# Four of nine depthwise taps moved from VectorE to TensorE, with the batch-norm columns on GpSimd and an early exponential, in a one-core metaformer kernel

## The reference, cut to what matters

```python
x1 = jnp.transpose(x, (0, 3, 1, 2))
x1 = lax.conv_general_dilated(x1, dw_k, (1, 1), [(PAD, PAD), (PAD, PAD)], feature_group_count=C)
x1 = bn_g[:, None, None] * (x1 - bn_m[:, None, None]) * lax.rsqrt(bn_v + 1e-05)[:, None, None] + bn_b[:, None, None]
x1 = jax.nn.silu(x1)
x1 = jnp.transpose(x1, (0, 2, 3, 1))
offset = x1 @ off_w + off_b
mask = jax.nn.softmax((x1 @ mask_w + mask_b).reshape(N, H, W, G, P), -1)
...
samples = _bilinear_sample(img, sg)
m = mask.reshape(N, H * W, G, P).transpose(0, 2, 1, 3).reshape(N * G, 1, H * W, P)
out = (samples * m).sum(-1)
```

## Time and profile before

| quantity | value |
|---|---|
| median of 3 runs | 272.5 us (272.42 to 273.59) |
| the profiled execution, its own time | 271.01 us |
| its span, first to last instruction | 268.9 us |
| mean granted TensorE clock | 0.924 of full speed |

### The profile page before, as it was taken

The page is one execution under the profiler, slowest core; times in us unless marked ns, Lnnn a source line. Parts: engine busy times, 40 slices in busy tenths (PEclk is TensorE's granted clock), DMA queues, the critical chain, the costliest instruction groups (busy, mean ns, idle before and its releaser), DMA issues.

```text
span 268.9 us, 3312 instructions
## 1 busy us (share of the span) xinstructions
PE 221.1 (82%) x1200; PEld 151.8 (56%) x1200; DVE 166.4 (62%) x412; ACT 55.9 (21%) x93; POOL 113.2 (42%) x150
## 2 busy tenths in 40 slices
PE   0968469898995889979794599999999869999980
PEld 0726167778993733224432289999999444334430
DVE  6796878996758286565414999966200354325496
ACT  1221944231000165424011101010102110211000
POOL 5600007999913309710800399997300020000760
PEclk9999959999999559999998589999999995999997
DMA  3547990000000000000029200000000000000000
GB/s 92 177 115 162 204 253 24 0 0 4 1 4 0 0 1 0 0 4 0 0 73 211 49 2 0 2 0 2 0 2 0 0 1 2 0 0 0 0 20 20
DMA packets 5825, 9.58 MB, mean 36 GB/s; under 512 B 2328, under 2 KB 2992, under 8 KB 5808
## 3 DMA queue, kind: packets, MB, share of 16 engines
q1 hardware_dynamic: 5808, 9.37, 14.8%
HBM read 7.67 MB, written 1.69 MB: 35 GB/s over the span
## 4 chain that ended last, share of the span: by engine, by line
PE 58%; DVE 24%; ACT 6%; issue 5%; POOL 4%; DMA 1%; DVEq 0%; POOLq 0%; ACTq 0%
PE ps L774 19%; PE ps L963 6%; PE ps L1031 6%; PE ps L757 4%; PE ps L702 3%; PE ps L917 3%; PE ps L832 3%; DVE cm L1143 2%; DVE xn L1099 2%; PE ps L854 2%; DVE ring L301 2%; POOL big L564 2%; PE ps L710 2%; DVE stats L1088 2%; DVE ps L1196 2%
## 5 line engine op out<-in xcount | busy, mean ns | idle before, releaser
L270 POOL TENSOR_TENSOR big<-big 128x576 f32<-128x576 f32 x32 | 36.3, 1176 | 21.5 <-DVE big L293 17.9
L757 PE MATMUL ps<-ring,ident 128*128 128x192 f32 x126 | 26.0, 357 | 8.6 <-DVE ring L301 8.4
L774 PE MATMUL ps<-ident,ring 128*128 128x128 f32 x256 | 32.7, 273 | 0.0
L270 DVE TENSOR_TENSOR ring<-big,ps 128x576 f32<-128x576 f32 x40 | 27.2, 749 | 5.5 <-PE ps L774 5.3
L311 POOL TENSOR_TENSOR big<-big 128x512 f32<-128x512 f32 x27 | 29.0, 1113 | 2.5 <-ACT big L631 2.4
L757 PEld LDWEIGHTS ps<-ring,ident 128*128 128x128 f32 x126 | 22.2, 205 | 12.8 <-DVE ring L301 12.8
L447 POOL TENSOR_TENSOR rstd<-veps,mhalf 128x4 f32<-128x4 f32 x8 | 8.2, 1028 | 49.6 <-DVE veps L1095 49.5
L774 PEld LDWEIGHTS ps<-ident,ring 128*128 128x128 f32 x256 | 28.9, 141 | 0.3 <-DVE ring L311 0.2
L774 PE MATMUL ps<-ident,big 128*128 128x128 f32 x212 | 27.7, 273 | 0.1
L774 PEld LDWEIGHTS ps<-ident,big 128*128 128x128 f32 x212 | 24.2, 141 | 1.3 <-POOL big L270 0.5
L702 PE MATMUL ps<-zero,ident 128*128 128x512 f32 x34 | 21.9, 793 | 2.8 <-DVE big L1436 2.8
(11 more groups left out here) (266 smaller groups left out, 334.8 us busy)
## 6 DMA issues: line engine op xcount, KB each, us to landing
big<-pad SPq DMA_DIRECT2D x8, 392.0 KB, 9.8
big<-pad SPq DMA_DIRECT2D x8, 240.0 KB, 5.4
w<-in_w_dram SPq DMA_DIRECT2D x2, 512.0 KB
w<-in_w_dram SPq DMA_DIRECT2D x2, 256.0 KB
pad<-img SPq DMA_DIRECT2D x8, 64.0 KB, 2.1
pad<-zero SPq DMA_DIRECT2D x1, 484.0 KB, 3.7
pad<-zero SPq DMA_DIRECT2D x1, 400.0 KB, 4.5
x<-in_x_dram SPq DMA_DIRECT2D x1, 256.0 KB, 2.8
```

Of the source, the lines that this page charges most:

```text
L270: return eng.tensor_tensor(term_slot(who, k, n * K * C, [3 * C1, 3], [C1, 3], [K * C1, G1], [1, C1]), bigv(dy * SLAB1 + (dx + j) * C, [SLA ...
L757: return mm(bank(px + dx, 0, P, [1, 3 * J * G0], off=dy * J * G0), ident[:, :], ring[:, slot + 3 * px * J * G0:slot + 3 * (px + 1) * J * G ...
L774: return mm(dst, columns, ident[:, :], is_transpose=True, start=first, stop=last, skip_group_check=True)
```

## The change

Taps 5 to 8 go to TensorE, taps 0 to 4 stay on VectorE. GpSimd builds four diagonal 128x128 weights in `w_shift`, a buffer that is used only much later. TensorE accumulates four multiplications in PSUM bank 4 on shifted views of `cpad`, and VectorE adds the bank to its own sum. `keep_clock` shrinks from four to one. The three batch-norm column instructions move from VectorE to GpSimd, ahead of the four memsets. ScalarE takes a one-column exponential right behind the SiLU.

```diff
-        warm = sb("warm", P, 1)
+        warm = sb("warm", P, 2)
...
+        dw_diag = w_shift
...
             pool.wait_ge(sem("bnv"), 1)
-            gp.tensor_tensor(bn[:, 1:2], bn[:, 0:1], mhalf[:, 0:1], ALU.pow).then_inc(sem("bnr"), 1)
+            step(gp.tensor_tensor(bn[:, 1:2], bn[:, 0:1], mhalf[:, 0:1], ALU.pow))
+            pool.wait_ge(sem("ident"), 1)
+            for q, tap in enumerate(PE_TAPS):
+                gp.tensor_scalar(dw_diag[:, q, :], ident[:, :], w_dc[:, tap:tap + 1], None, ALU.mult
+                                 ).then_inc(sem("dw_diag"), 1)
+            step(gp.tensor_tensor(bn[:, 2:3], w_dc[:, K:K + 1], bn[:, 1:2], ALU.mult))
+            step(gp.tensor_tensor(bn[:, 4:5], w_dc[:, K + 2:K + 3], bn[:, 2:3], ALU.mult))
+            gp.tensor_tensor(bn[:, 3:4], w_dc[:, K + 1:K + 2], bn[:, 4:5], ALU.subtract).then_inc(sem("bn"), 1)
             for weights in (w_i1[:, :, :], cw_parts[:, :, :], oh_parts[:, :, :], b1_parts[:, :]):
                 last = gp.memset(weights, 0.0)
...
                           bias=bn[:, 3:4], scale=bn[:, 2:3]).then_inc(sem("x1T"), 1)
+            sc.activation(warm[:, 1:2], mhalf[:, 0:1], ACT.Exp).then_inc(sem("exp_table"), 1)
...
             project(w_in[:, :], 2, C, "img0_ps", 1)
+            pe.wait_ge(sem("dw_diag"), len(PE_TAPS))
+            pe.wait_ge(sem("cpad0"), 1)
+            for n, tap in enumerate(PE_TAPS):
+                ky, kx = divmod(tap, 3)
+                last = mm(bank(4, 0, P, [1, 512]), dw_diag[:, n, :],
+                          V(cpad, 0, ky * (W + 2) + kx, [[1, P], [NP0, 2], [W + 2, H], [1, W]]),
+                          start=(n == 0), stop=(n == len(PE_TAPS) - 1))
+            last.then_inc(sem("dw_ps"), 1)
             pe.wait_ge(sem("zero_set"), 1)
-            keep_clock(4, 4)
+            keep_clock(1, 5)
...
-            step(last)
+            last.then_inc(sem("cpad0"), 1)
+            dve.wait_ge(sem("cpad0"), 1)
             n_dw = 15 * (W + 2) + W
-            for tap in range(K):
+            for q, tap in enumerate(DVE_TAPS):
                 ky, kx = divmod(tap, 3)
...
-                if tap == 0:
-                    step(v.tensor_scalar(dst, src, w_dc[:, 0:1], None, ALU.mult))
-                elif tap < K - 1:
+                if q == 0:
+                    step(v.tensor_scalar(dst, src, w_dc[:, tap:tap + 1], None, ALU.mult))
+                else:
                     step(v.scalar_tensor_tensor(dst, src, w_dc[:, tap:tap + 1], dst, ALU.mult, ALU.add))
-                else:
-                    v.scalar_tensor_tensor(dst, src, w_dc[:, tap:tap + 1], dst, ALU.mult, ALU.add).then_inc(sem("dwc"), 1)
-
-            dve.wait_ge(sem("bnr"), 1)
-            step(v.tensor_tensor(bn[:, 2:3], w_dc[:, K:K + 1], bn[:, 1:2], ALU.mult))
-            step(v.tensor_tensor(bn[:, 4:5], w_dc[:, K + 2:K + 3], bn[:, 2:3], ALU.mult))
-            v.tensor_tensor(bn[:, 3:4], w_dc[:, K + 1:K + 2], bn[:, 4:5], ALU.subtract).then_inc(sem("bn"), 1)
+            dve.wait_ge(sem("dw_ps"), 1)
+            rows = V(dwc, 0, 0, [[1, P], [H * (W + 2), 2], [W + 2, H], [1, W]])
+            v.tensor_tensor(rows, rows, bank(4, 0, P, [256, 2], [W, H], [1, W]), ALU.add).then_inc(sem("dwc"), 1)
...
+PE_TAPS = (5, 6, 7, 8)
+DVE_TAPS = (0, 1, 2, 3, 4)
```

## The result

The changed kernel takes 269.32 us (median of 4, 268.3 to 269.69) against 272.46 (median of 4): ratio 0.9876, interval 0.9844 to 0.9907. That is 3.1 us by the medians, where 2.7 and 269.8 us were forecast. Between the two profiled executions only 2.0 us went (271.01 to 269.06, spans 268.9 and 266.9), where the sum of the forecast was made for just this pair and said 3.1. Most of the difference between the two comparisons goes with TensorE's clock, as the experiments show.

What follows compares the result with a forecast made beforehand. The prediction took the head's chain of waits, from VectorE's taps through ScalarE's exponential to TensorE's table sums, as the bound: 1.46 + 1.30 + 0.3 = 3.1 us, less 0.4 for the median, gives 2.7 us, 269.8 us; range 267.5 to 271.9.

Steps and rivals of the forecast that it cites:

- case A: Whole kernel: the forecast holds, 2.0 to 3.4 us gained, 269.1 to 270.5 us; chance 0.5.
- The early exponential: ScalarE before the softmax exponential: the table load moves behind SiLU, hidden by a wait; 1.30 us gained.
- The taps: Head of the kernel: TensorE's taps end at 18.06, SiLU starts at 18.83 instead of 20.29; 1.46 us gained.
- the lower bound for it, 19.5: TensorE's taps: all eight instructions at the lower clock level take 6.8 us and end at 19.5.
- turn-by-turn estimate: VectorE's five taps alternating with GpSimd's memsets, constants and `b_out` addition: VectorE ends at 18.0.
- The collision: GpSimd's memsets and `b_out` addition beside VectorE's taps: hidden by TensorE's 18.06, counted as nothing; VectorE's end bounded by 16.43 and 19.9.
- The later slabs: Slab loads move by 3.9 us, GpSimd's first product starts at 43.25; costs nothing, at least 2.3 us of cover.
- Rival E: GpSimd's wait before its first product: the slabs become the bound and the kernel is slower, about 274 us; chance 0.07.
- point of decision: GpSimd's first product: starting after 45.6 (43.25 and 2.3 us of cover), each microsecond beyond costs one.
- L1204's contention: VectorE's product of two SBUF operands runs before GpSimd's slab products start; 0.3 us gained, bounds none to 0.5.
- The clock: TensorE's first table sums: a shorter idle time could gain 1.9 us or lose up to 1.3; nothing taken.
- Rival C: TensorE's first table sums: the clock doesn't fall in the shorter idle time, 1.9 us more, 267.9 us; chance 0.18.

Runs made afterwards that it cites:

- collision experiment: Changed kernel with GpSimd's memsets and constants moved into its early idle time and the `b_out` addition behind the `share` copy: 268.01 us, ratio 0.9871 to the kernel before.
- taps-alone profile: Changed kernel without the early exponential, leaving the tap split and moved batch-norm columns: 270.60 us, ratio 0.9978 to the kernel before.
- late-memset version: Changed kernel with GpSimd's memsets, constants and `b_out` addition held back until SiLU is done: 271.99 us, ratio 1.0002 to the kernel before.
- second one: Profile from the unaltered changed kernel run again on another chip with more executions: 268.40 us, ratio 0.9849 to the kernel before.
- six to three split: Changed kernel with six taps on VectorE, three on TensorE, GpSimd's memsets early and `b_out` addition late; without filler 267.24 us, ratio 0.9845 to the kernel before.
- the filler in the changed kernel: Changed kernel with three zero multiplications on TensorE behind the clearing of the tables: 267.19 us, ratio 0.9825 to the kernel before.
- the filler in the kernel before: Kernel before with four zero multiplications on TensorE behind the clearing of the tables, nothing else: 270.65 us, ratio 0.9948.
- version with both: Changed kernel with six VectorE and three TensorE taps, early memsets, late `b_out` addition and four zero multiplications behind the table clearing: 266.08 us, ratio 0.9746.

## Why the prediction was right

The forecast, 269.8 us and 269.1 to 270.5 for case A, met 269.32. Its terms can be checked on the two profiled executions, which have equal low time. The sum for them was 1.46 + 1.30 + 0.3 = 3.1; measured are 0.69 + 1.27 + 0 = 1.96, and the spans differ by 2.0. So the mechanism was right, two terms were too large, and the nearness of the median is partly luck, as told under the clock.

**The early exponential** was right in mechanism and size: 1.27 us from SiLU to the exponential, in the changed kernel and alone. The 2.66 us that the Trainium skill gives (ScalarE: Activation LUTs, section What ACT_TABLE_LOAD costs), which the row was weighed against, did not show.

**The taps** were right in mechanism, and the term of 1.46 us was mis-sized: 0.69 in the profiled execution. Two steps failed a little each. The clock rose later (the lower bound for it, 19.5, was nearly met in the collision experiment, 19.15), for which 0.4 had been taken off. And the turn-by-turn estimate of VectorE's end, 18.0, was 18.59, since the first tap waited for all the memsets. The collision, counted as nothing, was the later of the two bounds in the taps-alone profile (18.39 against 17.83), and would have been hidden in the profile without collision, where TensorE ended at 19.15; what it costs on average no run shows. Nor does a run move the batch-norm columns alone: the 0.5 us that they took on VectorE (19.79 to 20.25) is a part of the taps' term.

**The later slabs** cost nothing, as said, with the product start within 0.2 us of the forecast. Rival E is real behind its point of decision: in the late-memset version 4.81 us of wait. Its consumer was named wrongly, the first sum on VectorE instead of TensorE's seventeenth product being the one that waits. Its point of decision, a product start after 45.6, is near the 45.0 that this version shows.

**L1204's contention**, 0.3 us, did not go away in the first profile, since SiLU came 0.8 us later than forecast. In the second one, with SiLU at 19.38, it did (0.75 us), and the gain was lost again a few instructions later.

**The clock** is the term that was set to nothing and was not. With it at zero the sum for equal clocks should have been 2.4 or so (1.1 for the taps, 1.3 for the load); measured are 1.6. The remaining 1.5 to 2.2 us of the measured 3.1 and 3.8 go with the low time, of which executions of the changed kernel have less. About 1 to 1.3 us of that is the kernel before: its medians come from executions of its longer kind. The forecast of 269.8 met 269.32 partly because the two misses, taps too large and clock too small, cancel. Rival C named this and priced it well (1.9 against 2.05), but as a case with a single outcome; in truth the executions of the changed kernel differ in it, from 0.923 to 0.936.

Still open: why a shorter idle time leaves less low time in some executions and not in others, and why the exponential alone, with the same 4.8 us of idle time before the sums as the changed kernel, never ran above 0.924 in ten executions.

## What to carry to other kernels

Read how the mean clock of single executions sorts their times before comparing a profiled execution with a median; here a longer time at TensorE's lower clock went with 1.5 us, more than either part of the change. An engine that is idle ahead of a dense stretch costs there, not where it idles: filling that idle time was worth 0.5% in the kernel before and about 1% on top of the six to three split, though the clock fell in some of these executions all the same. When work moves to an engine that is cold, size its share at the lower clock, and look which writes of GpSimd come to lie beside VectorE's two-operand instructions.

## What the runs showed of the hardware

A VectorE multiplication by a scalar, 0.52 us alone, took 1.92 or 1.93 us beside a row of GpSimd memsets in four profiles and 1.12 in a fifth; so a GpSimd instruction without any input to read held VectorE up as well. Two VectorE instructions of one column took 0.92 and 1.00 us beside GpSimd's products, and 0.15 and 0.16 with GpSimd idle. The additions with one operand in PSUM took 0.69 us beside GpSimd's products (L1210) and with GpSimd idle (L1164 without the collision). TensorE's clock was at half for 37.6 us of both profiles that the forecast compares, and for 30.6 to 41.0 us in those of the other versions. It fell after work had already resumed behind 2.2 us of idle time in two profiles (the filler in the changed kernel, at 33.7; the filler in the kernel before, at 21.3). It stayed up behind 1.66 us in the version with both and behind 3.1 ahead of the offset matmuls in the kernel before, so the length of the idle time did not decide it alone.
